# The last stage of a decoder kernel: three-pass queries, biases on TensorE, an eight-largest operation, and a new order of the work

## What is computed

```python
# _L1_xattn_ref, its input x is the layer-normed row (called h in the kernel), e = 3
q_a = rope(heads(lin(x, W_qa, b_qa)));  q_t = rope(heads(lin(x, W_qt, b_qt)))   # 8 heads of 32
w = softmax(concat([q_a k_a, q_t k_t * gate]) / sqrt(32));  out = w @ concat([v_a, v_t])
x = lin(out, W_o, b_o) + x
xn = (x - mean(x)) / sqrt(var(x) + EPS) * gamma[e] + beta[e]
x = relu(lin(xn, W_ffn, b_ffn))
...
# _L1_ffn_ref, its input is the layer-normed sum
topw, sel = top_k(x @ Wg, 2);  topw = softmax(topw)          # 2 of 8 experts
h = einsum('td,edr->ter', x, A);  out = einsum('ter,erd->td', h * combine, B)   # rank 16 each
```

## Time and profile before

| | us |
|---|---|
| median of 3 runs | 2233.01 (2231.8 to 2234.94) |
| the profiled execution | 2229.74 |
| its span | 2228.0 |
| last stage, from its first DMA to the end | 1984.2 to 2228.0 |

### The profile page before, as it was taken

One profiled execution on the slowest core, in us unless ns is written; L12 is line 12 of the kernel. 1 busy time (PEld: TensorE's weight loads), 2 busy tenths in 40 slices (PEclk: granted clock), 3 DMA queues, 4 the chain that ended last, 5 costly groups with the idle time before them and its releaser, 6 DMA issues. The chain is left out here.

```text
span 2228.0 us, 54248 instructions
## 1 busy us (share of the span) xinstructions
PE 2038.8 (92%) x22301; PEld 1680.4 (75%) x22301; DVE 1418.3 (64%) x3131; ACT 1042.5 (47%) x2094; POOL 1003.7 (45%) x786
## 2 busy tenths in 40 slices
PE   6999999999999999679998679999999999948894
...
DMA packets 59988, 97.13 MB, mean 44 GB/s; under 512 B 7720, under 2 KB 50480, under 8 KB 57392
## 3 DMA queue, kind: packets, MB, share of 16 engines
...
## 5 line engine op out<-in xcount | busy, mean ns | idle before, releaser
L716 POOL TENSOR_TENSOR a_sm<-a_sm,a_rsum 128x1024 f32<-128x1024 f32 x256 | 484.8, 1894 | 390.3 <-DVE a_rsum L748 388.3
L736 DVE CUSTOM_DVE_ANT_0 a_sm<-psum,a_strip 128x1024 f32<-128x1024 f32 x256 | 312.1, 1219 | 57.9 <-PE psum L576 57.9
L655 ACT ACTIVATE a_sm<-a_sm,a_mn 128x1024 f32<-128x1024 f32 x256 | 293.4, 1146 | 25.2 <-DVE a_mn L736 25.1
L589 PEld LDWEIGHTS psum<-ident,a_sm 128*128 128x128 f32 x2048 | 220.0, 141 | 100.1 <-issue 92.0
L660 ACT ACTIVATE a_pT<-psum 128x512 f32<-128x512 f32 x256 | 152.9, 597 | 282.0 <-PE psum L589 281.8
L589 PE MATMUL psum<-ident,a_sm 128*128 128x128 f32 x2048 | 279.7, 280 | 4.7 <-POOL a_sm L716 4.7
L604 PE MATMUL psum<-a_pT,a_V 128*64 128x256 f32 x2048 | 249.0, 385 | 0.8 <-DVE a_pT L743 0.8
L743 DVE COPY a_pT<-psum 128x512 f32<-128x512 f32 x256 | 176.3, 689 | 100.6 <-PE psum L589 100.6
L604 PEld LDWEIGHTS psum<-a_pT,a_V 128*64 128x64 f32 x2048 | 135.8, 136 | 77.3 <-issue 20.7
L1746 ACT ACTIVATE g_val<-psum 128x512 f32<-128x512 f32 x64 | 38.1, 597 | 218.8 <-PE psum L1657 218.8
L1175 POOL TENSOR_TENSOR b_act_lo<-b_act,b_act_hi 128x512 fp32r<-128x512 f32 x64 | 87.7, 1375 | 91.2 <-ACT b_act_hi L1088 91.2
...
## 6 DMA issues: line engine op xcount, KB each, us to landing
...
b_oT_in<-oT SPq DMA_DIRECT2D x8, 1024.0 KB, 5.4
...
s_x<-in_x_rev SPq DMA_DIRECT2D x4, 512.0 KB, 7.5
...
```

The source lines that it names most:

```text
L589: last = pe.transpose(psum[:, 4 + j, k * P:(k + 1) * P], sm[:, st % RING, kt * P:(kt + 1) * P], ident[:, :])
L655: a.activation(sm[:, st % RING, :], sm[:, st % RING, :], ACT.Exp, scale=-1.0, bias=mn[:, at:at + 1], accum_out=rsum[:, at:at + 1]).then_in ...
L716: g.tensor_tensor(sm[:, st % RING, :], sm[:, st % RING, :], rsum[:, at:at + 1].broadcast_to([P, T]), ALU.mult).then_inc(sig("scaled"), 1)
L736: v.tensor_tensor_reduce(out=sm[:, st % RING, :], in0=scores_banks(hl).rearrange("p c n -> p (c n)"), in1=strip[:, pair % 2, hl, qt * P:qt ...
```

## The change

Only `context_and_low_rank` is changed.

- **Queries in three passes.** `wq` is split once into `wq2` (f32r, high and low; four pieces, `high_part` on ACT and `low_part` on DVE), `hT` for each part (`high_columns` on ACT, `low_columns` on DVE). An `eq` unit is now 12 f32r products instead of 4 f32 ones.
- **Biases on TensorE.** `b_o` and `b_ffn` are put into PSUM by a product of a constant matrix `mean` (1/64) with `bias` (rows 0 to 63 the high part, rows 64 to 127 the low part), one per tile, ahead of the f32 products of `ey` and `ew` (`biased_rows`). `hb` and `first_sum` are gone; DVE's addition of `b_ffn` too; the residual is added from `h`, which now has three buffers.
- **Gamma and beta** are applied as a scale and bias per partition when `gT` is copied out of PSUM (`scaled_columns`, two ACT operations of 128 x 256 in place of one of 128 x 512, or two on DVE in the last step). POOL's two passes over `y` are gone. The columns `gb` come from four transposes of `vec`, done once.
- **Eight-largest operation.** `two_best` takes `max` and `max_index` on the logits in PSUM, once per tile, in place of the comparisons; `weighted` holds the rest. `fl` has PSUM bank 7 for itself; the other units share seven.
- **Order.** `ey` of part `s` and `fT`, `fl` of part `s - 1` now stand at the end of step `s`; the queries of the next part are spread among the `ep` units. The step of the last part and the two behind it have a list of their own. `vec` is loaded after `cs`.

The core of the diff (eight blanks of indentation cut; the loops of the engines are shown by their order below):

```diff
 def order(s):
     every = [("es", s, n) for n in range(NU)] + [
-        ("eT", s + 1, 0), ("ey", s - 1, 0), ("fT", s - 2, 0), ("eq", s + 1, 0), ("eq", s + 1, 1),
-        ("eq", s + 1, 2), ("ep", s, 0), ("fl", s - 2, 0), ("ep", s, 1), ("eq", s + 1, 3), ("gT", s - 1, 0), ("ep", s, 2), ("ep", s, 3),
-        ("ew", s - 1, 0), ("eo", s, 0), ("fh", s - 2, 0), ("eo", s, 1), ("fo", s - 2, 0)]
+        ("gT", s - 1, 0), ("eT", s + 1, 0), ("ep", s, 0), ("ew", s - 1, 0), ("ep", s, 1), ("eq", s + 1, 0),
+        ("ep", s, 2), ("eq", s + 1, 1), ("ep", s, 3), ("eq", s + 1, 2), ("fh", s - 2, 0), ("eo", s, 0), ("eo", s, 1),
+        ("eq", s + 1, 3), ("fo", s - 2, 0), ("fT", s - 1, 0), ("ey", s, 0), ("fl", s - 1, 0)]
+    if s >= NP - 1:
+        every = [("es", s, n) for n in range(NU)] + [
+            ("ep", s, 0), ("gT", s - 1, 0), ("ep", s, 1), ("ew", s - 1, 0), ("ep", s, 2), ("ep", s, 3),
+            ("eo", s, 0), ("eo", s, 1), ("ey", s, 0), ("fh", s - 2, 0), ("fo", s - 2, 0),
+            ("fT", s - 1, 0), ("fl", s - 1, 0)]
     return [(stage, p, n) for stage, p, n in every if 0 <= p < NP]
 every_step = range(-1, NP + 2)
 per = {"eq": 4, "es": NU, "ep": NU, "eo": KC}
-units = [(stage, p * per.get(stage, 1) + n) for s in every_step for stage, p, n in order(s)]
-banks = Banks(sig, [psum[:, i, :] for i in range(8)], units)
+units = []
+for s in every_step:
+    units += [(stage, p * per.get(stage, 1) + n) for stage, p, n in order(s) if stage != "fl"]
+    if s < 0:
+        units += [("gb", 0)]
+banks = Banks(sig, [psum[:, i, :] for i in range(7)], units)
+ranked = Banks(sig, [psum[:, 7, :]], [("fl", s) for s in range(NP)])
...
                 pe.wait_ge(sig("eT_out"), s + 1)
-                pe.wait_ge(have("wq"), 16)
+                pe.wait_ge(sig("w_lo"), i + 1)
                 bank = banks.take(pe, "eq", n)
+                terms = passes(KC)
                 for m in range(KC):
-                    for k in range(KC):
-                        last = pe.matmul(bank[:, m * CP:(m + 1) * CP], wq[:, i, k, m * P:(m + 1) * P], hT[:, k, :],
-                                         start=k == 0, stop=k == KC - 1)
+                    for j, (wp, cp, k) in enumerate(terms):
+                        last = pe.matmul(bank[:, m * CP:(m + 1) * CP], wq2[:, i, wp, k, m * P:(m + 1) * P], hT[:, cp, k, :],
+                                         start=j == 0, stop=j == len(terms) - 1)
                 last.then_inc(sig("eq_ps"), 1)
...
+        def biased_rows(stage, s, cols, weight, row):
+            bank = banks.take(pe, stage, s)
+            for t in range(PT):
+                pe.matmul(bank[:, t * D:(t + 1) * D], mean[:, :], bias[:, row, :], start=True, stop=False)
+                for k in range(KC):
+                    last = pe.matmul(bank[:, t * D:(t + 1) * D], cols[:, k, t * P:(t + 1) * P], weight[:, k, :],
+                                     start=False, stop=k == KC - 1)
+            last.then_inc(sig(f"{stage}_ps"), 1)
...
+        def scaled_columns(s):
+            a.wait_ge(sig("gT_ps"), s + 1)
+            if s:
+                a.wait_ge(sig("ew_ps"), s)
+            else:
+                a.wait_ge(sig("gb_out"), 1)
+            for k in range(KC):
+                last = a.activation(gT[:, k, :], halves(banks("gT", s))[:, k, :], ACT.Identity,
+                                    scale=gb[:, 0, k:k + 1], bias=gb[:, 1, k:k + 1])
+            last.then_inc(sig("gT_out"), 1)
...
+        def residual(s):
+            v.wait_ge(sig("ey_ps"), s + 1)
+            if s:
+                v.wait_ge(sig("gT_ps"), s)
+            v.tensor_tensor(y[:, :, :], tiles_of(banks("ey", s)), h[:, s % HR, :, :], ALU.add).then_inc(sig("ey_out"), 1)
+            v.wait_ge(sig("ey_out"), s + 1)
+            norm_stats(v, sig, "yn", s, y, yn)
+        def rectified(s):
+            v.wait_ge(sig("ew_ps"), s + 1)
+            if s > 1:
+                v.wait_ge(sig("fo_out"), s - 1)
+            v.scalar_tensor_tensor(x5[:, s % 2, :, :], tiles_of(banks("ew", s)), 0.0, x[:, s, :, :],
+                                   ALU.max, ALU.add).then_inc(sig("ew_out"), 1)
+            v.wait_ge(sig("ew_out"), s + 1)
+            norm_stats(v, sig, "fn", s, x5[:, s % 2, :, :], fn)
...
+        def two_best(s):
+            v.wait_ge(sig("fl_ps"), s + 1)
+            ranks = tiles_of(ranked("fl", s))
+            for t in range(PT):
+                chain(v.max(best[:, t, :], ranks[:, t, E0 * R:E0 * R + E0]))
+            v.tensor_tensor(gap[:, :], best[:, :, 1], best[:, :, 0], ALU.subtract).then_inc(sig("f_gap"), 1)
+            for t in range(PT):
+                chain(v.max_index(at[:, t, :], best[:, t, :], ranks[:, t, E0 * R:E0 * R + E0]))
+            chain(v.tensor_scalar(place[:, :, :], at[:, :, 0:2], -1.0, float(E0), ALU.mult, ALU.add))
+            for i, part in enumerate((one, second)):
+                chain(v.tensor_tensor(part[:, :, :], over_tiles(rev[:, :], PT), spread(place[:, :, i], E0), ALU.is_equal))
```

270 lines of the change are left out of this document (164 added, 106 removed).

## The result

| | before | after |
|---|---|---|
| median, us | 2233.75 (4 runs, 2231.8 to 2234.94) | 2209.24 (4 runs, 2207.51 to 2209.96) |
| ratio | | 0.989, 95% interval 0.9873 to 0.9907 |
| profiled execution | 2229.74, span 2228.0 | 2209.78, span 2208.0 |

The change makes the kernel 24.5 us faster; the forecast was 30.0 faster. In the two profiled executions the spans differ by 20.0 only. The last stage, from its first load of rows to the end of the span, took 243.8 us before and 218.6 after, 25.3 less, but in the execution of after it started at 1989.44 where it had started at 1984.18. Where no number of runs is given, an experiment is one profiled execution, and it is read by the stretches of its trace and not by its whole time.

The account below looks back on a forecast made before the run. No engine alone bound it: work passed from VectorE to ScalarE to TensorE in turn. Terms -17.7 - 0.8 - 0.9 - 5.6 - 5.2 + 0.2 = -30.0 gave 2199.7 from 2229.74; the median, 3.3 above, 2203.0 us; range 2194 to 2217.

Parts of the forecast that it names:

- Rival A: Every step: VectorE's queue binds, as `ey` must precede the next maxima; 2 us more per step, about 2216; chance 0.15.
- C: Queries: f32r products among f32 ones lose their rate, adding 5.2 us per step, 2245 at worst; chance 0.04.
- D: Whole kernel slower: 4.5 us of waits per step, at ScalarE's queue, eat the gains; chance 0.03.
- E: Middle steps stay at 24.5 us, with the ends as reckoned: 2221 us; chance 0.05.
- first scores after 2009: Start of the last stage: a sign that the forecast is wrong; first scores were expected at 2006.6 us.
- Middle steps: Five middle steps: 21.0 us each, from 20.35 of TensorE work and 0.5 to 1.0 of waiting; 122.7 to 105.0, -17.7.
- Part 0: First part: 17.2 to 16.4 us, losing 1.5 of queries and some waits, gaining `ey` (2.0); -0.8.
- Part 1: Second part: stays 19.1 us, losing 1.5 of queries, gaining 0.5 of biases and 1.4 of `fT`, `fl`; 0.
- Last part: Scores to `ey` of the last part, 21.2 us before with 4.25 of waiting: `ey` at 15.6, -5.6.
- `ew` until 10.0: Last part's chain: `ew` ends 10.0 us after the first score product, leading to `ep` 3 at 13.0.
- Behind it: From the last `ey` to the last store's data: 31.4 to 26.7 us, -4.7, taken as -5.2.
- Start: Stretch before the first scores: these come at 2006.6 us, -0.9, between -2.5 and +2.

Follow-up runs that it names:

- the two parts put alone into it: Kernel before with only the eight-largest operation added: middle steps 23.06 us, 1.5 less each; with only the three-pass queries: 0.8 longer on average, profiled execution 2236.2 us.
- the repetition: The changed kernel run once more, unedited: median 2211.45 us of 5 runs, ratio 0.9906 to the kernel before; its last stage took 215.9 us.
- `inverse` first: Changed kernel with VectorE's second reciprocal put ahead of the scaling of transposed rows in the last step: scores to `ey` 16.3 us, whole end 44.1 us.
- the held clock: Changed kernel with unread transpositions of the identity in TensorE's waits of the last steps: clock 1.00, last scores to last output tile 39.4 us.

## Why the prediction was right, and where it was not

**Right by the mechanism, in the main.** The kernel before was read as a chain from engine to engine, with TensorE not the bound; the two parts put alone into it (-1.5 and +0.8 per step) show that. The links were not all the right ones: the chain of the profile goes from TensorE's scores through VectorE and GpSimd, and ScalarE's copy of `hT` is not on it. Nor did VectorE's stretch of 1.4 us go because GpSimd lost three passes; it had run beside the products with the probabilities, which stayed, and the order parted them. That number was right by luck. The waits in the middle fell to 0.5 us per step, the lower end of "0.5 to 1.0". Rival A did not come: the loop closes with VectorE waiting 1.4 us for `ey`. The 1.53 us of a unit exclude C, the steps of 20.4 exclude D and E. One of the signs of being wrong, first scores after 2009, did come (2011.64), but the stage had started 5.3 us late; counted from the first load they were early.

**Middle steps, -17.7 forecast, -20.6 measured.** The step that was mis-sized is "20.35 us per step" of TensorE's work plus "0.5 to 1.0 of waiting". Work was 19.90, waiting 0.52. A unit of queries holds TensorE for 1.53 us and not 1.46, so these are not where the 0.45 us came from. Most of them lie in the 21.39 that the prediction started from. In one of the five steps of the profile before the granted clock fell to about 0.8 between 2114 and 2122, and there the scores took 4.57 us instead of 3.72 and the product with `fb` 1.91 instead of 1.13: 1.6 us, or 0.3 per step. The kernel before with the eight-largest operation alone, which gives TensorE the same work at a clock of 1.00, was busy for 105.2 us and not 106.9. The rest is in groups that stood behind a wait or were split (scores 3.72 against 3.62, the output products 1.28 against 1.07); no run separates this. VectorE's "about 18 us" was 17.76. `gT` with scale and bias took 1.06 us where 1.0 was taken.

**Part 0, -0.8 forecast, -0.1 measured.** And that with the clock's help: before, part 0 ran at 0.91, after at 1.00. In the repetition, again at 0.91, it took 18.17 us, 1.1 more than before. So at equal clock the 2.0 us of `ey` outweighed what queries and waits gave back; which of the terms is off was not tested.

**Part 1, 0 forecast, +2.0 measured.** The step that failed is the one that summed TensorE's units and left the queues out. `gT` was moved ahead of the queries, and the prediction did not ask what stands ahead of its input on GpSimd in that one step: 4.04 us of clears. With them moved, 1.7 came back.

**Last part, -5.6 forecast, -1.7 measured.** Two things. "`ep` 3 at 13.0" was 15.3, and in its sum the step that failed is "`ew` until 10.0": it ended at 12.3, and from there the chain took what was forecast. `ew` was late because the second group of transposes is ahead of it, and the reciprocal for that group stands behind VectorE's scaling, which waits 1.12 us for a transposition; the prediction placed ScalarE's operations one by one and gave VectorE only those it needed. And `ew` itself took 3.4 us where it takes 2.1 in a middle step. With the two operations exchanged, and `ew` at the higher level, the group came at 12.05. The rest is the clock: the same waits gave 19.55 and 18.03 us in two executions.

**Behind it, -5.2 forecast, -3.75 measured.** "`gT` starts at 5.6" was 8.6: 2.2 us because `ey` ran at the low level (1.91 us for four products, not 1.02), and 0.8 because `y`, applied at 2179.3, had to wait until TensorE was done with `fT` and `fl` of part 6, started at 2177.8. From `gT` on it took 19.0 us where the prediction had 21.1, since `ew` met the higher level there (2.1 us, forecast as 3.64 and the biases). The two errors, +3.0 and -2.1, nearly cancel, so this term looks better than it was. The allowance of 1.5 for "a clock that has less time to fall" had the right subject and the wrong width: the clock alone moves this end by 4 us between executions, and by 8 (47.2 to 39.4) when it is held. From the last logits to `hw` it took 3.4 us (2191.71 to 2195.10), as forecast (3.5).

**Start, -0.9 forecast, -1.15 measured**, and the end, where four more clears show nothing. Left open: whether `inverse` first and the held clock add up in the order of its own, and what lets the clock return in one execution and not in the next, from the same work.
